# Plain fp32 for the scatter, the first aggregation and the filter net, fp32r with hi and lo columns for the gather

## The reference

```python
h = relu(layernorm(x)); x = x + adj_normalised @ (h @ W0) + bias          # layer 0
h = relu(layernorm(x))                                                    # layer 1
hs = xs @ w_s / sqrt(128);  hv = einsum(xv, w_v) / sqrt(128)              # 32 + 3*32 channels a node
s, v = hs[dst], hv[dst]                                                   # gather to the edges
Wf = (ssp(f_ij @ W1 + b1) @ W2 + b2) * rcut                               # filters, 4 of 6 are used below
edge = [s*ys*Wf0, sum(v*yv)/sqrt(3)*Wf1, s*yv*Wf2, v*ys*Wf3, ...]         # 8 of 16 rows reach the output
agg = segment_sum(edge, src)                                              # scatter to the nodes
x = x + small dense layers of agg
```

## Time and profile before

| | us |
|---|---|
| median of 3 runs | 76.31 (76.28 to 79.52) |
| profiled execution | 76.64 |
| its span | 74.8 |
| TensorE busy in the span | 67.6, 475 matmul records |
| VectorE busy | 58.8 |
| ScalarE busy | 36.9 |
| GpSimd busy | 29.1 |
| granted clock of TensorE | 1.0 over the span |

### The profile page before, as it was taken

One profiled execution on the slowest core, in us unless ns is written; L12 is line 12 of the kernel. 1 busy time (PEld: TensorE's weight loads), 2 busy tenths in 40 slices (PEclk: granted clock), 3 DMA queues, 4 the chain that ended last, 5 costly groups with the idle time before them and its releaser, 6 DMA issues.

```text
span 74.8 us, 1309 instructions
## 1 busy us (share of the span) xinstructions
PE 67.6 (90%) x475; PEld 55.4 (74%) x475; DVE 58.8 (79%) x135; ACT 36.9 (49%) x62; POOL 29.1 (39%) x35
## 2 busy tenths in 40 slices
PE   3996989999999879899999999999999999999630
PEld 1242466488643448799999999999999999998520
DVE  4657999999395999999399999949495959982570
ACT  0600389400922876938434457757737484822600
POOL 4000000007986500191009797791938585600000
PEclk9999999999999999999999999999999999999999
DMA  0899999870000000000000000000000000000035
GB/s 6 175 367 252 394 476 437 347 247 12 0 0 0 0 0 0 0 4 0 0 9 0 0 0 0 0 0 0 13 0 0 0 0 0 0 0 0 9 112 169
DMA packets 3050, 5.66 MB, mean 76 GB/s; under 512 B 540, under 2 KB 1936, under 8 KB 2916
## 3 DMA queue, kind: packets, MB, share of 16 engines
q1 hardware_dynamic: 2274, 5.14, 19.6%
q10 hardware_dynamic: 770, 0.44, 2.1%
HBM read 5.06 MB, written 0.52 MB: 75 GB/s over the span
## 4 chain that ended last, share of the span: by engine, by line
PE 65%; DVE 11%; DMA 8%; ACT 5%; issue 5%; SPq 1%; POOL 1%
PE bank L644 21%; PE bank L628 20%; PE bank L512 8%; DMA f_sb<-f_t 8%; PE bank L560 4%; PE bank L538 4%; PE bank L520 3%; PE bank L605 2%; PE bank L557 2%; DVE hW_lo L412 2%; DVE hX L409 2%; DVE x L419 1%; ACT za L196 1%; ACT h L233 1%; ACT za L240 1%
## 5 line engine op out<-in xcount | busy, mean ns | idle before, releaser
L644 PE MATMUL bank<-OsR,Mh 128*128 128x256 f32 x68 | 16.8, 287 | 0.0
L644 PE MATMUL bank<-OsR,Ml 128*128 128x256 f32 x68 | 16.5, 284 | 0.0
L628 PE MATMUL bank<-H,OdT 128*128 128x128 f32 x136 | 16.5, 275 | 0.0
L628 PEld LDWEIGHTS bank<-H,OdT 128*128 128x128 f32 x136 | 15.9, 192 | 0.0
L335 POOL TENSOR_TENSOR Ml<-dst_bc,Mh 128x512 fp32r<-128x512 f32 x8 | 10.3, 1286 | 12.2 <-ACT Mh L267 12.2
L644 PEld LDWEIGHTS bank<-OsR,Ml 128*128 128x128 f32 x68 | 12.9, 190 | 0.0
L644 PEld LDWEIGHTS bank<-OsR,Mh 128*128 128x128 f32 x68 | 12.8, 188 | 0.0
L512 PEld LDWEIGHTS bank<-OdT,Os 128*128 128x128 bf16 x68 | 7.0, 105 | 3.6 <-DVE OdT L350 1.3
L512 PE MATMUL bank<-OdT,Os 128*128 128x256 bf16 x68 | 9.4, 298 | 0.1
L267 ACT ACTIVATE Mh<-dst_bc 128x512 fp32r<-128x512 f32 (+1 forms) x9 | 5.5, 607 | 7.9 <-DVE dst_bc L464 7.9
L339 POOL TENSOR_TENSOR Ml<-dst_bc,Mh 128x512 fp32r<-128x512 f32 x7 | 9.0, 1292 | 0.0
(11 more groups left out here) (109 smaller groups left out, 111.4 us busy)
## 6 DMA issues: line engine op xcount, KB each, us to landing
dst_bc<-dst_row SPq DMA_DIRECT2D x1, 2176.0 KB, 13.2
w_sb<-w SPq DMA_DIRECT2D x1, 1024.0 KB, 8.4
x_sb<-x SPq DMA_DIRECT2D x1, 512.0 KB, 4.8
out<-x_sb SPq DMA_DIRECT2D x2, 192.0 KB, 1.9
f_sb<-f_t SPq DMA_DIRECT2D x1, 378.0 KB
b_sb<-bias SPq DMA_DIRECT2D x1, 256.0 KB, 13.3
w_sb<-w ACTq DMA_DIRECT2D x1, 128.0 KB, 4.3
out<-x_sb ACTq DMA_DIRECT2D x1, 128.0 KB, 1.9
```

The costliest lines, as they stand in the source:

```text
L628: last = nc.tensor.matmul(gbank[g % RG][:, j * C:(j + 1) * C], OdT[:, a, t * P:(t + 1) * P], H[:, a, :], start=(a == 0), stop=(a == NH - 1))
L644: last = nc.tensor.matmul(bank[4 + b][:, 0:N], part[:, g % RG, j, feats(b)], OsR[:, g % RG, j, :], start=(t == 0 and part is Mh), stop=(t ...
```

## The change

The scatter multiplies `M` and `OsR` as plain fp32: one matmul for each tile and half, no `Mh` and `Ml`. `OsR` holds all tiles; its second half shares memory with `Od`, so that its copies wait for the adjacency. `M` has four slots instead of three. The gather has its one-hots and `H` in fp32r, the rounded part and the rest of `H` as two sets of 128 columns side by side (`HL`), 256 moving columns for each matmul, in a pair of PSUM banks, of which there are two. ScalarE copies the first set to SBUF (`S_sb`), VectorE adds the second; the rest of the message is computed from there. The first aggregation has plain fp32 `A` and `hW`. The filter net handles three tiles at a time with the bias as a 97th row: one plain fp32 matmul with 384 columns for three tiles, twelve in all; ScalarE copies the results to `Wsb`, two of the four filters with a scale of `y`. The b2 input is gone. Of f and x, SP issues f first. Tiles 6 to 11 of the adjacency now stand ahead of the transposes of `h1`, and all four steps of the first half of the first layer ahead of tile 28. VectorE takes over the square of `h2`'s second half.

```diff
-    RG = 3
+    RG = 2
+    RM = 4
+    TF = 3
+    NF = (T + TF - 1) // TF
...
-        OdT = sb("OdT", [P, NH, E])
-        Od = OdT[:, 0, :].bitcast(bf16).rearrange("p (t n) -> p t n", t=T)
-        OsR = sb("OsR", [P, RG, TG, N], fp32r)
+        OdT = sb("OdT", [P, NH, E], fp32r)
+        OsR = sb("OsR", [P, T, N])
+        Od = OsR[:, T // 2:, :].bitcast(bf16).rearrange("p t (k n) -> p (t k) n", k=2)
...
             sp.dma_start(idx_sb[:], idx).then_inc(d_idx, 16)
+            sp.dma_start(f_sb[:], f_t).then_inc(d_f, 16)
             sp.dma_start(x_sb[:, :, :], x.rearrange("(a p) d -> p a d", p=P)).then_inc(d_x, 16)
-            sp.dma_start(f_sb[:], f_t).then_inc(d_f, 16)
...
+            def filters_out(i):
+                act.wait_ge(q["y"], 1)
+                act.wait_ge(q["W"], i + 1)
+                t0, n = TF * i, ftiles(i)
+                nc.scalar.activation(Wsb[:, t0:t0 + n, 2:4, :], filters_of(i)[:, :, 2:4, :], ACT.Copy)
+                for t in range(n):
+                    last = nc.scalar.activation(Wsb[:, t0 + t, 0:2, :], filters_of(i)[:, t, 0:2, :], ACT.Copy,
+                                                scale=y[:, t0 + t, 0:1])
+                last.then_inc(q["Wsb"], 1)
+            for g in range(4):
+                scatter_onehots(g)
             act.wait_ge(q["scales"], 1)
+            act.wait_ge(q["hW"], 1)
+            nc.scalar.activation(hW[:, 0, :], bank[0], ACT.Copy, scale=s1[:, 0:1]).then_inc(q["hWs"], 1)
+            filters_out(0)
+            filters_out(1)
             act.wait_ge(q["wc"], 1)
...
             for g in range(NG):
-                nc.scalar.activation(Mh[:, o, 0:n, feats(1)], M[:, o, 0:n, feats(1)], ACT.Copy).then_inc(q["MhB"], 1)
-                act.wait_ge(q["MA"], g + 1)
-                nc.scalar.activation(Mh[:, o, 0:n, feats(0)], M[:, o, 0:n, feats(0)], ACT.Copy).then_inc(q["MhA"], 1)
+                act.wait_ge(q["G"], g + 1)
+                if g >= RG:
+                    act.wait_ge(q["svw"], g - RG + 1)
+                    act.wait_ge(q["msg"], g - RG + 1)
+                nc.scalar.activation(S_sb[:, g % RG, 0:n, :, :], rows_of(g)[:, :, 0, :, :], ACT.Copy).then_inc(q["Ghi"], 1)
+                if 4 + g < NG:
+                    scatter_onehots(4 + g)
+                if 6 + g < NF:
+                    filters_out(6 + g)
...   # VectorE
+            dve.wait_ge(q["hW"], NH)
+            nc.vector.tensor_scalar(hW[:, 1, :], bank[1], s1[:, 1:2], None, ALU.mult).then_inc(q["hWs"], 1)
+            node_onehots(0, 0)
...
+                nc.vector.tensor_tensor(sv.rearrange("p t c f -> p t (c f)"), sv.rearrange("p t c f -> p t (c f)"),
+                                        rows_of(g)[:, :, 1, :, :].rearrange("p t c f -> p t (c f)"),
+                                        ALU.add).then_inc(q["add"], 1)
+                dve.wait_ge(q["add"], g + 1)
+                dve.wait_ge(q["Wsb"], (t0 + n - 1) // TF + 1)
...   # TensorE
-            adjacency(range(0, 2))
-            adjacency(range(2, 6))
+            adjacency(range(0, 6))
             for c in range(3):
                 hidden(c)
+            adjacency(range(6, 12))
...
-            first_layer(0, 0, 1)
-            adjacency(range(6, 12))
-            first_layer(0, 1, 3)
-            adjacency(range(12, T))
-            first_layer(0, 3, KD)
+            adjacency(range(12, 20))
+            first_layer(0, 0, 2)
+            adjacency(range(20, 28))
+            first_layer(0, 2, KD)
+            adjacency(range(28, T))
...
+            filters(0)
+            filters(1)
+            for a in range(NH):
                 for b in range(NH):
+                    pe.wait_ge(q["hWs"], NH)
+                    last = nc.tensor.matmul(bank[4 + a], A[:, b, a * P:(a + 1) * P], hW[:, b, :],
+                                            start=(b == 0), stop=(b == NH - 1))
+                last.then_inc(q["L0"], 1)
+            ...   # wc
+            filters(2)
             transposes(0)
             transposes(1)
+            filters(3)
             node_channels(0)
             node_channels(1)
             filters(4)
+            filters(5)
...
+                    pe.wait_ge(q["add"], g - RG + 1)
                 for j in range(tiles(g)):
                     for a in range(NH):
+                        last = nc.tensor.matmul(gpair[g % RG][:, j * 2 * C:(j + 1) * 2 * C], OdT[:, a, t * P:(t + 1) * P],
+                                                HL[:, a, :, :], start=(a == 0), stop=(a == NH - 1))
...
+                pe.wait_ge(q["svw"], g + 1)
+                pe.wait_ge(q["msg"], g + 1)
+                for b in range(NH):
                     for j in range(tiles(g)):
-                        for part in (Mh, Ml):
-                            last = nc.tensor.matmul(bank[4 + b][:, 0:N], part[:, g % RG, j, feats(b)], OsR[:, g % RG, j, :],
+                        last = nc.tensor.matmul(bank[4 + b][:, 0:N], M[:, g % RM, j, feats(b)], OsR[:, t, :],
+                                                start=(t == 0), stop=(t == T - 1))
```

More of the change, by code:

```diff
@@ L96, in gnn_preln_kernel @@
         CI = sb("CI", [P, NH, N], bf16)
-        A = sb("A", [P, NH, N], fp32r)
+        A = sb("A", [P, NH, N])
         deg = sb("deg", [P, 2 * NH])
@@ L100, in gnn_preln_kernel @@
         dinv, s1 = scales[:, 0:NH], scales[:, NH:2 * NH]
-        hW_hi = sb("hW_hi", [P, NH, D], fp32r)
-        hW_lo = sb("hW_lo", [P, NH, D], fp32r)
+        hW = sb("hW", [P, NH, D])
         x1 = sb("x1", [P, NH, D])
@@ L108, in gnn_preln_kernel @@
         s2 = sb("s2", [P, NH])
[L109 to L116, removed]
+        HL = sb("HL", [P, NH, 2, C], fp32r)
+        za = sb("za", [P, NF * P])
         y = sb("y", [P, T, 4])
         warmup = sb("warmup", [P, 512], bf16)
[L119 to L124, removed]
+        Wsb = sb("Wsb", [P, T, 4, F])
+        S_sb = sb("S_sb", [P, RG, TG, 4, F])
+        M = dst_bc[:].bitcast(fp32)[:, 0:RM * TG * S * F].rearrange("p (o t n) -> p o t n", o=RM, t=TG)
         aggT = sb("aggT", [P, 2, N])
@@ L129, in gnn_preln_kernel @@
         warm = sb("warm", [P, 1])
-        bank = [ctx.enter_context(nc.psum_tensor(f"bank{i}", [P, 512], fp32)) for i in range(8)]
+        pair = [ctx.enter_context(nc.psum_tensor(f"pair{i}", [P, 1024], fp32)) for i in range(4)]
+        bank = [pair[i // 2][:, 512 * (i % 2):512 * (i % 2) + 512] for i in range(8)]
         bT = bank[2][:, :].bitcast(bf16)
-        (d_x, d_idx, d_dst, d_f, d_yr, d_w0, d_b0, d_w1, d_w2, d_b2, d_win, d_o1s, d_o1v, d_o2s, d_o2v,
+        (d_x, d_idx, d_dst, d_f, d_yr, d_w0, d_b0, d_w1, d_w2, d_win, d_o1s, d_o1v, d_o2s, d_o2v,
          d_out) = [sem("dma_" + n) for n in
-                         "x idx dst f yr w0 b0 w1 w2 b2 win o1s o1v o2s o2v out".split()]
+                         "x idx dst f yr w0 b0 w1 w2 win o1s o1v o2s o2v out".split()]
         names = ("half warmup iota eye idp st mv1 ve h1 tp1 h1T hW "
[L138 to L142, removed]
+                 "onehot adj CI CT A degve scales hWs L0 xb x1 "
+                 "h2 neg_h2 tp2 h2T0 h2T sq0 sq1 ve2 s2 H Hh Hl "
+                 "z zabs zexp zln hT one W Wsb "
+                 "y OdT OsR "
+                 "G Ghi add m0 vys sw2 vyv svw red msg scat "
                  "scatA aggA aggT wc wcs o1 os1 ta te tl rl os1T fin os2 ov o")
@@ L151, in gnn_preln_kernel, with filters_of, rows_of @@
         zb = (bank[2], bank[3], bank[7])
[L152 to L158, removed]
+        gpair = (pair[0], pair[3])
+        fbank = [bank[(3, 2)[i % 2]] for i in range(NF)]
+        def filters_of(i):
+            n = ftiles(i)
+            return fbank[i][:, 0:n * P].rearrange("p (t k f) -> p t k f", t=n, k=4)
+        def rows_of(g):
+            return gpair[g % RG][:, 0:tiles(g) * 2 * C].rearrange("p (t h c f) -> p t h c f", t=tiles(g), h=2, c=4)
         def feats(b):
@@ L234, in _ @@
                                  scale=-float(D)).then_inc(q["neg_h2"], 1)
[L236 to L251, removed]
+            act.wait_ge(q["neg_h2"], 1)
+            nc.scalar.activation(hW[:, 0, :], h2[:, 0, :], ACT.Square, accum_out=sq[:, 0:1]).then_inc(q["sq0"], 1)
+            act.wait_ge(q["tp2"], 1)
+            nc.scalar.activation(h2T[:, 0, :, :], bank[6], ACT.Relu, scale=-1.0).then_inc(q["h2T0"], 1)
+            filters_out(2)
+            filters_out(3)
             act.wait_ge(q["s2"], 1)
@@ L292, in _ @@
             nc.gpsimd.memset(neghalf[:], -0.5).then_inc(q["half"], 1)
-            nc.gpsimd.memset(ones[:], 1.0).then_inc(q["ones"], 1)
+            pool.wait_ge(q["half"], 2)
+            nc.gpsimd.memset(za[TF * F:TF * F + 1, :], 1.0).then_inc(q["one"], 1)
             pool.wait_ge(q["onehot"], len(WAVES))
+            pool.wait_ge(q["one"], 1)
             pool.wait_ge(d_b0, 16)
@@ L540, in first_layer, with filters @@
                     last.then_inc(q["hW"], 1)
-            def filters(g):
-                n = tiles(g)
-                if g == 0:
```

(61 more changed lines are left out.)

203 lines of the change are left out of this document (63 added, 140 removed).

## The result

The changed kernel took 92.8 us (median of four executions: three of 91.95 to 93.21 us and one of 202.85), and the three took 1.210 times the kernel before [1.195, 1.225]. Forecast were 87.4, with 84.7 to 89.8 as the range: the direction was right, the size 5 us short, outside the range. In the execution of 202.85 us TensorE's groups of records, the warm-up's too, took 2.5 to 2.8 times as long as at full clock; it is left out of what follows, and its cause stays open.

What follows compares the result with a forecast made beforehand. TensorE's instruction stream was taken to bound the edge loop. Loop +7.3, hole +1.0, ahead of the loop +3.0 and end -0.2 gave +11.1 us, so 87.4 us on the footing of the 76.31 median; range 84.7 to 89.8.

Steps and rivals of the forecast that it cites:

- The loop, +7.3 us: Edge loop on TensorE: scatter +13.3 us, gather -7.0, filters +1.0; VectorE and ScalarE stay covered.
- The hole ahead of scatter(0): Start of the edge loop: TensorE waits 1.05 us for the message of group 0, at most twice that.
- x lands at 7.6: Front loads: with f issued first on SP's queue, x lands at about 7.6 us instead of 5.96.
- The term that hung on it, +2.6 us on adj: Ahead of the loop: late one-hots of tiles 6 to 11 move the adjacency's end from 19.9 to 22.5 us.
- the clock: Rival: TensorE idles 2 to 3 us before tile 6, its clock falls, adjacency at half pace, +1.5 us; chance 0.12.
- The rest of the front: From the adjacency's end to gather(0): first aggregation +0.8 us, then -0.4 up to gather(0).
- The end, -0.2: After the last scatter: the longer scatter covers the aggT copy that L662 waited for, -0.2 us.

Runs made afterwards that it cites:

- the scatter's run: The kernel before with only its scatter changed to plain fp32 from M, without Mh and Ml: ratio 1.171, which is 89.6 us.
- the kernel with its front repaired: Changed kernel with w2 in 128 rows, x first, the front's old order and five warm-up matmuls ahead of the hidden layer: 87.12 us, ratio 1.139.
- the loop with one fp32r part: Changed kernel with M and the scatter's one-hots in fp32r, one matmul each, what M has beyond fp32r left out: 84.4 us, ratio 1.095.

## Why the prediction was wrong

- **The loop, +7.3 us:** right. Scatter, gather and filters at their forecast prices, TensorE without idle time, VectorE covered; confirmed alone by the scatter's run, 89.6 for 89.5.
- **The hole ahead of scatter(0):** 1.19 us for 1.05, but gather(0) to scatter(0) was 6.1 us for 5.2. ScalarE's copy of group 0 began at 43.54, right behind filters_out(4) and (5), some 0.4 us after the gather's end. From there the copy took 0.8 us to the addition (0.6 forecast), the addition 0.7 (0.6) and the rest of the message 3.1 to scatter(0) (2.7). The rows at the end of this section show who ended the waits.
- **The step that failed: x lands at 7.6, "the bytes of the two together are the same".** It summed the bytes of SP's queue and left out the rows of the loads beside them. The term that hung on it, +2.6 us on adj, was measured as +7.0 (27.0 against 20.0). Two things were missing. First, w2's 97 rows: x came at 9.2, of which 1.1 us go with w2's rows and 0.5 stay open.
- **Second, the clock**, held as a rival at 0.12 and priced at 1.5. The forecast stood on an idle time of 2 to 3 us; it became 4.7, and the clock cost 2.3 us on adj (27.0 to 24.7). Rival and forecast were not exclusive, and the chance of 0.12 was too low even for an x at 7.6: the clock also fell in the run with w2 in 128 rows and x first, behind an idle time of 1.6 us. The argument that "no row of before shows a fall" rested on one execution, and others of the same kernel had mean clocks down to 0.942.
- **The rest of the front:** adj to gather(0) 15.0 us for 15.4; adj itself 0.5 later than x and the clock explain.
- **The sum of the miss:** 1.6 + 2.3 + 0.5 - 0.4 + 0.9 + 0.1 = 5.0 us, for 91.0 - 85.9 = 5.1 in the span. That the kernel with its front repaired takes 87.1, close to the 87.4 forecast, is partly chance: its adj ends at 21.1, 1.4 earlier than the forecast's, and the loop's start takes 0.9 more.
- **The end, -0.2:** right; L601 follows the scatter's last record at 85.13 at once.

```profile
42.95 0.75 ACT L223 ACTIVATE Wsb<-pair,y 128x64 f32<-128x64 f32 x3
43.54 0.65 ACT L258 ACTIVATE S_sb<-pair 128x512 f32<-128x512 f32 x1
...
44.33 0.69 DVE L410 TENSOR_TENSOR S_sb<-S_sb,pair 128x512 f32<-128x512 f32 x1 [1.17 <-ACT S_sb L258]
48.12 3.69 PE L583 MATMUL pair<-OsR,dst_bc 128*128 128x256 f32 x16 [1.19 <-DVE dst_bc L432]
```

## What to carry to other kernels

Where TensorE is the bound, price a rewrite in its records and moving columns: one plain fp32 matmul of 256 columns (0.43 us) costs almost twice two fp32r ones (0.24), and what it saves elsewhere was free. Look at the number of rows of every load that a change reshapes, not only at its bytes and order. Fill short waits of TensorE early in a kernel with matmuls that nobody reads, and read the granted clock of several executions before calling it safe.

## What the runs showed of the hardware

- 1.5 us of idle time ahead of the hidden layer, in a front that was not dense before it, was followed by the clock's fall from 2.4 to 1.2 GHz for 10 us; filled with 1.2 us of matmuls it stayed up. Waits of 1.19 and 1.24 us at the same place in kernels with the front of before did not lower it.
- TensorE, busy for 4.7 of the 8 us from 62 to 70 in the loop with one fp32r part, also lost its clock (0.50 from 70 us on), though it never stood still there for more than 1.9 us.
- A load of 97 rows instead of 128 went with a landing 15 us later of the 85 KB behind it and, on another queue, 1.1 us later of x and 3.9 of W0.
- A record with 128 columns costs 0.109 us as fp32r and 0.111 as one of the two of fp32; one with 256 columns costs 0.119 as fp32r and 0.216 as one of the two of fp32.
